# Shared experts in float16 parts ahead of the routed ones, weights streaming past held slots, the first tiles combined while slots come in

## The reference, cut to what matters

```python
logits = x @ gate_w.T                    # 32 experts in 8 groups; 3 groups kept, 6 experts a token
...
slot = jnp.where(valid, flat_e * C + pos, E * C)        # C = 48 slots an expert, filled in token order
buf = jnp.zeros((E * C + 1, h), x.dtype).at[slot].set(x[tok_idx])
gu = jnp.einsum('ech,ehf->ecf', xb, w_gate_up)          # per expert 48 x 256 @ 256 x 352
act = jax.nn.silu(g) * u
yb = jnp.einsum('eci,eih->ech', act, w_down)            # 48 x 176 @ 176 x 256
...
out = jnp.einsum('tk,tkh->th', topk_w, y_pairs)         # back to the tokens that have a slot
gs, us = jnp.split(x @ ws_gate_up, 2, axis=-1)          # shared experts, every token, 352 wide
out = out + jax.nn.silu(gs) * us @ ws_down
```

## Time and profile before

| | us |
|---|---|
| median of 3 runs | 1713.99 (1712.78 to 1716.14) |
| the profiled execution | 1712.16 |
| its span, first to last instruction | 1710.3 |
| conv and MLP stage, up to | 394.5 |
| routing and shared experts, up to the first routed expert | 517.5 |
| routed experts among the shared ones, up to the last | 632.6 |
| slots back and combine, up to the attention's first instruction | 679.3 |
| PE busy in the span | 85% |
| mean granted TensorE clock | 0.939 |

### The profile page before, as it was taken

One profiled execution on the slowest core, in us unless ns is written; L12 is line 12 of the kernel. 1 busy time (PEld: TensorE's weight loads), 2 busy tenths in 40 slices (PEclk: granted clock), 3 DMA queues, 4 the chain that ended last, 5 costly groups with the idle time before them and its releaser, 6 DMA issues.

```text
span 1710.3 us, 26008 instructions
## 1 busy us (share of the span) xinstructions
PE 1459.0 (85%) x9810; PEld 817.1 (48%) x9811; DVE 1143.0 (67%) x2288; ACT 737.5 (43%) x1241; POOL 239.5 (14%) x249
## 2 busy tenths in 40 slices
PE   3999999976989996459888888888988888998897
PEld 2666666654557876213334443343533344433355
DVE  5666666647421124688948789859879679789475
ACT  5555555511312220416765126754137752157630
POOL 3344444411330000100011000010000110000000
PEclk8999999987999988659999999999999998999998
DMA  2000000006013420332101022212023101112100
GB/s 113 13 26 25 25 25 25 25 13 196 13 42 116 152 89 26 101 62 38 32 17 33 8 38 45 44 29 34 1 44 57 44 20 25 35 32 40 32 1 25
DMA packets 137484, 75.23 MB, mean 44 GB/s; under 512 B 117648, under 2 KB 126352, under 8 KB 136592
## 3 DMA queue, kind: packets, MB, share of 16 engines
q1 hardware_dynamic: 136800, 72.02, 17.4%
q0 software_dynamic: 576, 1.77, 0.4%
HBM read 37.59 MB, written 9.06 MB: 27 GB/s over the span
## 4 chain that ended last, share of the span: by engine, by line
issue 57%; POOL 3%; DVE 0%; POOLq 0%; DVEq 0%
POOL rs_sb L1446 1%; POOL xs_sb L1452 1%; POOL ve_sb L1443 0%; POOL qks_sb L1466 0%; DVE bn_sb L1627 0%; DVE x_sb_sb L1661 0%; POOL v_sb L1464 0%; POOL qks_sb L1456 0%; POOLq L66 0%; POOLq L1159 0%; DVE mv_sb L1633 0%; DVEq L1159 0%; POOL v_sb L1463 0%; POOL qks_sb L1467 0%; DVE ident_h_sb L1844 0%
## 5 line engine op out<-in xcount | busy, mean ns | idle before, releaser
L1526 ACT ACTIVATE room_sb<-s_ps 128x1024 f32<-128x1024 f32 (+1 forms) x320 | 292.3, 941 | 161.6 <-PE s_ps L2006 157.3
L1712 DVE TENSOR_REDUCE mx_sb<-s_ps 128x1 f32<-128x512 f32 (+1 forms) x400 | 249.5, 651 | 56.5 <-PE s_ps L1982 34.0
L1979 PE MATMUL s_ps<-room_sb 48*128 48x512 f16 (+3 forms) x480 | 145.3, 340 | 32.3 <-DVE mx_sb L1707 20.3
L2026 PE MATMUL cm_ps<-room_sb,v_sb 128*32 128x512 f32 (+3 forms) x1536 | 157.0, 496 | 1.0 <-ACT room_sb L1532 0.8
L2006 PE MATMUL s_ps<-room_sb 51*128 51x128 f16 (+4 forms) x1152 | 136.3, 273 | 14.6 <-ACT room_sb L1526 10.8
L2131 PE MATMUL cm_ps<-w_fd_sb,room_sb 128*128 128x256 f32 x512 | 130.8, 404 | 12.6 <-DVE room_sb L1790 12.6
L1443 POOL TENSOR_TENSOR ve_sb<-mv_sb,eps_sb 128x4 f32<-128x4 f32 x24 | 5.2, 216 | 886.7 <-DVE mv_sb L1633 833.6
L396 DVE SCALAR_TENSOR_TENSOR x_sb_sb<-xp_sb,conv_w_sb,x_sb_sb 128x512 f32<-128x512 f32 x96 | 106.6, 1113 | 22.6 <-ACT x_sb_sb L319 20.5
L1979 PEld LDWEIGHTS s_ps<-room_sb 48*128 48x128 f16 x480 | 41.8, 94 | 152.6 <-DVE mx_sb L1712 77.6
L2131 PEld LDWEIGHTS cm_ps<-w_fd_sb,room_sb 128*128 128x128 f32 x512 | 97.2, 198 | 36.4 <-issue 14.0
L2118 PE MATMUL s_ps<-xbT_sb,w_fg_sb 128*128 128x512 f16 x384 | 101.1, 393 | 8.4 <-DVE ctok_sb L1760 7.7
(11 more groups left out here) (268 smaller groups left out, 2947.5 us busy)
## 6 DMA issues: line engine op xcount, KB each, us to landing
we_gu_sb<-we_gu SPq DMA_DIRECT2D x32, 352.0 KB
we_dn_sb<-we_dn SPq DMA_DIRECT2D x32, 176.0 KB
x_in_sb<-x SPq DMA_DIRECT2D x9, 512.0 KB, 3.5
rows<-x_sb_sb SPq DMA_DIRECT2D x8, 512.0 KB, 3.0
x_sb_sb<-rows SPq DMA_DIRECT2D x2, 2048.0 KB, 11.3
out<-x_sb_sb SPq DMA_DIRECT2D x8, 512.0 KB, 3.0
room_sb<-qks_sb SPq DMA_TRANSPOSE x88, 3.3
xp_sb<-w_in SPq DMA_DIRECT2D x1, 1024.0 KB, 5.6
```

Of the source, the lines that this page charges most:

```text
L1526: act.activation(weights[(g * NU + u) % SLOTS_P][:, 2 * pair:2 * pair + 2, 0:width(u) * P], W[s % 2][:, :, 0:width(u) * P], ACT.Exp, scale ...
L1712: dve.tensor_reduce(mx[:, pair, k % 2, slot:slot + 1], max_bank(g, m)[:, 0:count * P], AX.X, ALU.max, negate=True).then_inc(mx_ok, 1)
L1979: last = pe.matmul(bank[:, at * P:(at + plain) * P], query[head:head + NORM, i * P:(i + 1) * P], key[head:head + NORM, j * P:(j + plain) * ...
L2026: last = pe.matmul(O[32 * h:32 * h + 32, (i - half * GT) * P:(i - half * GT + count) * P], v[:, j, g * HG + h, :], weights[(g * NU + u) % ...
```

## The change

Five things change, all before the attention.

1. The shared experts work on float16 parts. `xT` becomes two float16 tensors, made in the first stage by ACT (high) and POOL (rest); the weights are loaded and split during that stage; `shared_chunk` makes each chunk from 2 x 3 float16 matmuls and `down` each tile from 3 x 3. DVE makes silu(g)*u in float32 (`product`), ACT its high part (`high`), POOL (groups 0 to 2) or DVE the rest (`low`).
2. Four chunks of group 0 are made at the end of the first stage, before the last layernorm is turned; the `product`s and `low`s of groups 0 to 4 stand between the routing steps on DVE; counting moves from group 2 to group 3, turning the gathered rows from group 5 to group 7.
3. The routed experts all come after the shared ones. `expert_gu` holds the 48 slots and streams 352 columns of weights past them, two matmuls an expert; the result has slots on partitions, so `expert_turned` turns it on PE and DVE copies it out. `expert_down` follows two experts later.
4. The one-hot matrices of the first eight tiles are made in pieces of a quarter between the experts, in float16.
5. The barrier before the combine is gone. As soon as a chunk of slots is turned back and scaled, PE sums it into the first four tiles; then come the next four.

```diff
+def shared_chunk(pe, mm, keep, g, c):
+    for k in range(KD):
+        for wp, xp in PRODUCTS:
+            last = pe.matmul(mm[c % 4][:, :], ws_gu[wp][:, k, col:col + P], xT[xp][:, k, g * GTOK:(g + 1) * GTOK],
+                             start=(k == 0 and wp == xp), stop=(k == KD - 1 and xp == 1))
...
-                    pool.tensor_copy(xT[:, :, bass.ds(c(GTOK), GTOK)], xaT[:, :, :]).then_inc(xT_ok, 1)
+                    pool.tensor_tensor(xT[1][:, :, own], xaT[:, :, :], xT[0][:, :, own], ALU.subtract).then_inc(xT_ok, 1)
...
+                    act.activation(xT[0][:, :, bass.ds(c3(GTOK), GTOK)], tp[:, :, :], ACT.Copy).then_inc(xTh_ok, 1)
...
                         wait(pe, h1Tl_ok, NG)
+                        shared_first()
...
-                    wait(pool, x1_ok, b(2, 2))
+                    wait(pool, h1_ok, b(1, 1))
...
+            def expert_gu(e, k):
...
+                    wait(pe, ring[e % RING], 32 * (e // RING + 1))
+                    wait(pe, ea_ok, e - 1)
+                last = pe.matmul(tp[e % 2][0:CAP, 0:2 * IN], xgT[:, k, e, :], we_gu[:, e % RING, k, :],
+                                 start=(k == 0), stop=(k == KD - 1))
...
+            def expert_turned(e):
+                wait(pe, ea_ok, e + 1)
+                wait(pe, ec_ok, e - 1)
+                for k in range(NIX):
+                    last = pe.transpose(mm[e % 2][0:IX, k * CAP:(k + 1) * CAP], ea[:, e % 2, k * IX:(k + 1) * IX], ident[0:CAP, 0:CAP])
...
+            for e in range(E + 2):
+                for k in range(2):
+                    if e < E:
+                        expert_gu(e, k)
+                    if k == 1 and 1 <= e <= E:
+                        expert_turned(e - 1)
+                    if e >= 2:
+                        expert_down(e - 2, k)
...
+            slot_out(0)
+            slot_out(1)
             for j in range(CJ):
+                first_quad(j)
+                if j + 2 < CJ:
+                    slot_out(j + 2)
+            for r in quads(pe):
...
```

More of the change, by code:

```diff
@@ L702, in _, with turns @@
+        def turns(g):
+            for i in range(TURNS):
+                chunk, tile = (i, None) if i < EARLY else (None, i - EARLY) if i < LATE else (i - GT, None)
+                if (chunk is not None and g < NG) or (tile is not None and g > 0):
+                    yield i, chunk, tile
+        block = ctx.enter_context(nc.Block())
         @block.sync
         def _(sp):
-            for src, dst in (("ws_gu", ws_gu), ("ws_dn", ws_dn), ("upper", upper), ("ones", ones), ("ones_f", ones_f),
-                             ("place", place), ("mine", mine), ("lane", lane), ("base", base)):
+            for src, dst in (("upper", upper), ("ones", ones), ("ones_f", ones_f), ("place", place), ("mine", mine), ("lane", lane), ("base", base)):
@@ new lines, in _ @@
+            for g in range(NG + 1):
+                for i, c, t in turns(g):
+                    if c in (0, 2, 4):
+                        gate(g, c // 2)
+                    if t in (1, 3):
+                        down(g - 1, t // 2)
+                    if g < NG and i >= LATE:
+                        high(g, i - LATE)
+                    if g == 2 and i == LATE - 1:
+                        act.wait_ge(rt, CENTERED)
+                        act.activation(ex, ex, ACT.Exp).then_inc(exp_ok, 1)
@@ new lines, in _ @@
+            for r in quads(dve):
+                among = r.reg is None
+                for i in range(0 if among else QUAD):
+                    dve.wait_ge(cb_mm, r(1))
+                    dve.tensor_tensor(hot[i][:, :, :], rel[:, bass.ds(r(1, i), 1), :].rearrange("p a j -> p (a j)")
+                                      .unsqueeze(2).to_broadcast([P, CJ, P]),
+                                      lane[:, :].unsqueeze(1).to_broadcast([P, CJ, P]), ALU.is_equal).then_inc(oh_ok, 1)
+                for i in range(QUAD):
+                    dve.wait_ge(cb_mm, r(1, i + 1))
+                    added(i, total[r.off // QUAD][i], r)
@@ new lines, in combined, with first_quad @@
+            def combined(i, j, bank, of):
+                for half in range(2):
+                    last = pe.matmul(bank, hot[of][:, j, :], y[half][:, j, :],
+                                     start=(j == half == 0), stop=(j == CJ - 1 and half == 1))
+                if j == CJ - 1:
+                    last.then_inc(cb_mm, 1)
+            def first_quad(j):
+                wait(pe, y_ok, j + 1)
+                for i in range(QUAD):
+                    combined(i, j, total[0][i], i)
+            for g in range(NG + 1):
+                for i, c, t in turns(g):
+                    if c is not None and (g > 0 or c >= 4):
+                        gate_up(g, c)
+                    if t is not None:
+                        down(g - 1, t)
+                    if g == SLOTS_AT and t == 0:
+                        pe.wait_ge(cnt_ok, 1)
+                        pe.wait_ge(cum_ok, NG)
+                        pe.matmul(tp[0][0:1, 0:NT], ones_f[:, 0:1], busy_f[:, :], start=True, stop=True).then_inc(busy_mm, 1)
+                    for m in slots_at(g, i):
+                        if m == 0:
+                            pe.wait_ge(busy_ok, 1)
+                            pe.wait_ge(gath, 16 * CJ)
+                        slot_features(m)
+                    if g == COUNT_AT and t == GT - 1:
+                        counted()
@@ L1096, in _ @@
+            for r in quads(pe):
+                if r.reg is None and r.off == 0:
+                    continue
+                for i in range(QUAD):
+                    if r.reg is not None:
+                        pe.wait_ge(oh_ok, r(1, i + 1))
+                        pe.wait_ge(cb_ok, r(1))
                     for j in range(CJ):
-                        for half in range(2):
-                            last = pe.matmul(total[i], hot[i][:, j, :], y[half][:, j, :],
-                                             start=(j == half == 0), stop=(j == CJ - 1 and half == 1))
```

460 lines of the change are left out of this document (243 added, 217 removed).

## The result

The changed kernel takes 1749.47 us (median of four executions, 1742.24 to 1752.76) against 1713.38 us (1707.31 to 1716.14): ratio 1.021, 95% interval 1.0167 to 1.0252. It is slower. The forecast was 1679 us, and the range ended at 1708. The profiled execution took 1742.24 us, the shortest of the four, with a mean granted clock of 0.915; the other three show 0.905 to 0.907.

A forecast was written before the change was run, and what follows sets the result against it. TensorE was taken to bound shared and routed experts, a DVE-TensorE chain the combine. First expert -3.5, experts -17, combine -15 gave -35 us: 1712.2 to 1677, plus 1.8 for the median, 1679 us; range 1660 to 1708.

The forecast's parts named there:

- Routed experts: Stretch from first to last routed expert: 98 us against 115.1, so -17 us; bounds 92 and 113.
- the wait (0.7 us in a turn): Among the routed experts, TensorE waits 0.7 us in each turn for DMA, as the ring has four places.
- Its formula: Routed experts: two turns last 2.3 us of work plus 3.75 us for the load, one turn 3.03 us.
- estimate of 3.24 us for the load: Skill page's figure for a 528 KB load, giving turns of 2.87 us; the forecast kept the trace's row instead.
- The same in full, slower than before: All 32 routed experts at the low clock level: +50 us, about 1730 us; chance 0.07.
- 352 columns stream where 48 did: Argument against the clock falling among the routed experts, where each slow expert was priced at 1.55 us.
- First routed expert: End of the shared stage: first routed expert starts at 514 us against 517.5, so -3.5; bounds 500 and 524.
- DVE holds the shared experts longer: Shared stage: more products or POOL's parts come late, first routed expert at 524 or later, 1690 us; chance 0.10.
- the down product of group 3: Shared stage: its last input is ready at 456.2 us, held by DVE's routing steps and products.
- the first stage, counted as unchanged: Stage before the barrier: no change in its length, bounds -2 to +3 us.
- the gathered rows: Turning them on TensorE within group 7 of the shared experts adds 8.4 us, priced from group 5 before.
- Combine: From the routed experts to the attention: 32 us against 46.7, so -15 us; bounds 28 and 44.

The follow-up runs named there:

- experiment 1: Changed kernel with six places for experts' weights instead of four: 1686.85 us, ratio 0.9837 to the kernel before.
- 5: Changed kernel with six weight places, but expert 16's load held back as with four: 1724.95 us, ratio 1.0085 to the kernel before.
- 6: Changed kernel with six weight places, expert 16's load held back one turn longer than with four: 1732.06 us, ratio 1.0117 to the kernel before.
- experiment 9: Changed kernel with six weight places, one long wait before expert 16, and 24 unread float16 matmuls at expert 20: 1711.76 us, ratio 0.9992.
- 4: Changed kernel with the gathered rows turned in six places of four instead of three of eight: median 1744.5 us.
- 8: Changed kernel with six weight places, gathered rows turned in six fours, DVE copying them before its products and low parts: 1680.27 us, ratio 0.9818.
- kernel 11: Changed kernel with six weight places, rows turned in six fours and copied first, and 128 held columns in `expert_gu`: 1668.30 us, ratio 0.9735.
- 2: Changed kernel, four weight places kept, with `expert_gu` holding 128 columns instead of 48: median 1723.3 us of ten executions.
- 10: Changed kernel with six weight places, one long wait before expert 16, and 128 held columns in `expert_gu`: 1691.20 us, ratio 0.9865.
- 12: As kernel 11, with `expert_gu` of the first two experts ahead of the last group's down product: 1699.09 us, ratio 0.9916.

## Why the prediction was wrong, point by point

*Routed experts, the step that failed.* The forecast found the wait (0.7 us in a turn) and priced it only as itself. Its formula was near: pairs of 6.85 us against 6.05, as a turn's own work was 2.81 us and not 2.3 (by the starts, `expert_gu` 1.45 us against 1.18 and `expert_down` 1.15 against 0.89), and from the end of `expert_down` to the use of the place's new weights it was about 4 us (533.62 to 537.66) and not 3.75. That is some 10 us over 32 experts. (The page "DMA: Bandwidth & Descriptors" of the Trainium skill, section "Anatomy of one DMA", had led, by a fit on another kind of queue, to an estimate of 3.24 us for the load; the trace, with its 4 us, does not bear it out.) The other 39 are the clock: 24 turns at 5.03 instead of 3.4 us. Experiments 1 and 5 show that the wait is the cause of the fall; 6 shows that the turns with 48 held columns do not undo it, and 9 that a burst of other matmuls does.

*The rival that came true.* "The same in full, slower than before", with a chance of 0.07 and 1730 us. I held against it that 352 columns stream where 48 did. That was an argument about keeping the clock, and the turns do keep it; what I left out is the way back. In the kernel before, the clock fell too, not once but three times among the experts (554.94, 612.58 and 627.51 us), each time behind a wait of only 0.51 or 0.52 us for ACT; five more such waits there passed. This is the second:

```profile
612.58 1.42 PE L992 MATMUL et_ps<-maps_sb,we_gu_sb 128*88 128x48 f32 x16 [0.51 <-ACT arena_sb L783]
...
614.74 2.76 PE L975 MATMUL er_ps<-ws_dn_sb,su_sb 128*128 128x256 f32 x6
```

After the first two, shared matmuls between the experts followed, and the level was 1.2 GHz for a few us; the change took away just these. That they bring the clock back is read from these rows and fits the burst of experiment 9; no run of the kernel before tests it. The Trainium skill's rule ("TensorE: Matmul & The Clock Gate", section "HAM oscillation — how this bites in real kernels"), that a loop which waits for DMA in each turn is throttled again in each turn, pointed the right way, and I gave it too little weight. The Trainium skill tells it of waits of 3 to 5 us. The trace differs from it in two things: waits of 0.51 us (for ACT) and 1.40 us were enough here, and throttled once, these turns waited no more and still stayed at 0.50 for 121.9 us.

*First routed expert, 527.5 against 514.* The rival "DVE holds the shared experts longer" came true as well. That the down product of group 3 began as forecast (456.61 us against 456.2) was luck, as two errors cancel: the first stage, counted as unchanged, ended some 5 us earlier than before (first load behind the barrier issued at 389.39 us against 394.46; last turnings at 383.63 us against 387.17), and DVE's routing steps took that back. The two rows:

```profile
383.63 1.09 PE L501 MATMUL tp_ps<-ident_sb,x_sb_sb 128*128 128x128 f32 x8 [0.36 <-DVE x_sb_sb L489]
...
456.61 5.77 PE L1100 MATMUL er_ps<-ws_dn_sb,su_sb 128*128 128x256 f16 x36 [2.23 <-DVE su_sb L895]
```

Behind it, the gathered rows were priced at 8.4 us with a row in which DVE had little else to do (three up chunks of 0.69 us). With DVE's products and low parts between they took 20.9 us with three chunks (about 12 forecast), and the last down product, most of it at the low level, 6.50 us instead of 4.09. Experiments 4 and 8 won 4.2 and then 3.4 us of it by order alone.

*Combine, 32.7 us against 32.* Right. From 680 us a chunk takes TensorE 1.17 us (1.2 forecast), and from the last add to the attention it is 4.2 us. This time the clock came up with its first float16 matmuls:

```profile
680.21 0.38 PE L1156 MATMUL et_ps<-ident_sb,arena_sb 128*128 128x128 f32 x2
680.43 0.60 PE L1162 MATMUL er_ps<-y_sb,sg_sb 128*128 128x256 f16 x4
...
702.82 0.42 DVE L1067 TENSOR_TENSOR x_sb_sb<-et_ps,x_sb_sb 128x256 f32<-128x256 f32 x1 [2.19 <-PE et_ps L1162]
...
707.44 0.10 POOL L1569 MEMSET power_sb<- 128x4 f32 x1 [176.79 <-POOLq L657]
```

*The forecast's sum in the end.* With the wait gone (experiment 1) the kernel takes 1687 us, 8 above the forecast, and kernel 11 takes 11 less than it. The nearness of the 1687 us is in part luck: the first routed expert comes 13 us late (527.1 against 514), and the experts take 8 us less than forecast (90.4 against 98).

Left open: what besides its length decides whether a wait drops the clock (of three waits of 1.05 to 1.40 us the first two passed and the third did not, and of eight of about 0.51 us in the kernel before three did not), and why 128 held columns bring the clock back after 13 us in one kernel, some 40 in another and 110 in a third. Which instruction of a turn counts for the way back was not taken apart.

## What to carry to other kernels

Price a new wait on TensorE not by its length but by what follows it: if the loop behind it cannot regain the clock, one wait of 1.8 us cost some 38 us. So before dense work is moved out from between thin matmuls, make the loads deep enough that nothing waits, and hold the full 128 columns where the extra rows are free. A price read where an engine had little else to do doesn't hold where the change gives it more.

## What the runs showed of the hardware

- The two levels of the clock have memory here: the turns with 48 held columns ran on at 1.00 almost without a gap (89.76 of 90.4 us busy, experiment 1), and as well at 0.50 with no gap (121.9 us, the changed kernel). With 128 held columns, same streamed count, they came up from 0.50 by themselves in each of the three traces where they fell to it (experiments 2, 10 and 12).
- A wait of about 0.5 us dropped the clock in three of eight cases among the experts of the kernel before; in the kernel of experiment 11 one of 2.37 us did not.
- Holding 128 columns instead of 48 made a turn shorter, 2.49 against 2.81 us (experiments 10 and 1), though it loads more; by their starts, four instructions of `expert_down` take 0.38 to 0.48 us behind the wide `expert_gu` and 0.57 behind the narrow one.
- DVE's subtraction of 128x512 float32 into float16 took 2.42 us where it ran beside POOL's addition (501.06 to 503.40 us), and 0.67 to 0.69 elsewhere in that kernel; in experiment 4 it was 2.22 us beside the addition, in experiment 8, behind it, 0.67.
